# Scale and shift of every modulation in two halves of the columns, in a four-stream transformer kernel

## The chip, the cores and the metric

The kernel runs on one core of one Trainium2 chip. The metric is the device time of one execution in microseconds. TensorE is called PE in the rows (PEld its weight loads), VectorE DVE, ScalarE ACT, GpSimd POOL and SyncE SP.

## The reference

The input `x` is 128 sequences of 32 tokens of 128 features; `cond` is one row of 128 features for each sequence. Four layers follow one another. Layer 0 is a graph attention in two directions over the first 20 tokens as keys. Layers 1 and 3 each have an attention block and an MLP block with 512 hidden features; layer 2 has two MLP blocks, with 128 and 256 hidden features. Each of these six blocks begins with a layer norm and a modulation whose scale and shift come from `cond`:

```
xn = _layernorm(x, g, be)
xm = xn * (1.0 + sc[:, None, :]) + sh[:, None, :]
x  = x + gt[:, None, :] * block(xm)      # attention, or gelu(xm @ W1 + b1) @ W2 + b2
```

## The kernel before

The 128 sequences are cut into 8 chunks of 16 sequences, 512 tokens each (`C` = 512 columns, `NB` = 16 sequences of `S` = 32). Four streams (`NS` = 4) have their own buffers and PSUM banks; stream s does chunk s and then chunk s + 4. All matrices are fp32.

Every engine has a list of stages written out as a string of digits in `MERGE`: each digit says which stream's next stage comes (4 is the setup). An engine takes its list strictly in order and waits on semaphores; so a stage that waits holds up all that is behind it on that engine. Six blocks (`BLOCKS`, index 0 to 5; 0 and 4 are attention, 1, 2, 3 and 5 are MLPs) make 48 modulations in the 8 chunks, 32 of them for MLPs.

The way of one chunk through the beginning of a block:

- `stats` on VectorE (L886 to L893), then on GpSimd the reciprocal root (L637) and L639
- `norm` on ScalarE, four 128x128 activations (L736), each transposed by TensorE into the bank `xn` (L1037)
- `modulate` on VectorE (L899): features times scale, 128x512, from PSUM into the tile `turned_in` (called `xm0` here)
- `modulate` on GpSimd (L644): plus shift, into the tile `xm`. For an attention block the columns are written in another order (`keys_order`)
- on TensorE, for an MLP, `hidden` u = 0, 1, ... (L1058): 128x512 matmuls of one weight tile each, two passes in the trace, so that the 88 hidden matmuls are 176 entries; for an attention block `keys` (q at L973, k at L976) and `vals` (L981)
- GELU on ScalarE (L741), `down` on TensorE (L1067, 32 entries for 512 hidden features), gate and residual on VectorE (L905, L908). GpSimd adds the gated bias to x in `base` (L623).

In attention, TensorE does many small matmuls (`scores` L1009, `values` L1024), VectorE adds, takes maxima and subtracts (L847, L851, L854, L856) and transposes (L862), ScalarE does the exponentials (L727), and the divide by the row sums is L866 and L870. ScalarE loads another function table where exp, gelu and tanh-gelu follow one another; such a load is named ACT_TABLE_LOAD at the line of the activation that needs it.

Of the kernel before, what the change touches and what calls it, by code (L numbers as in the profile page):

```python
# [10 lines left out]
ALU = mybir.AluOpType  # L11
# [3 lines left out]
P = 128  # L15
B, S, D = 128, 32, 128
# [130 lines left out]
def order(engine, merge):  # L147
# [2 lines left out]
    return [next(turns[int(s)]) for s in merge]  # L150

MERGE = {
    "tensor": ("001014414042420420132021030023021022201210212122011212121230230023023132323013113203022223321003"
               "231313120132000010113231132230120303321332021300102312310123021020230112100333012022213220331212"
               "312103200001032020230132021311201120302102113201333033021301230210113231310303102313031333310112"
               "210023213303012122223012100003303213111101302023331331201222030101123132020201320331302211232031"
               "33123021202103321323010000013111313333"),
    "vector": ("001014441442204200330120220201200212212201202210121011312012213233231023203032033301332321302011"
               "130112231303023303122310021033101023122023321102210023020233100132012101031133120021132320233203"
               "112022332020122033021001100100313013321123131313133013223300021302211102031303322113010332013102"  # L160
               "01232310122310021103323122023320031221132013013303011203310313"),
    "scalar": ("444444041440440412440212000312222001112221122303202013333201102332222103213301230010023111103223"
               "021330332210031023211002310201133022322101332212300010320220201310113200012113333120301211323031"
               "330302123310110321330122202231300002131101130231333021223010211302120302332101320133123230221230"
               "10003011113333"),
    "gpsimd": ("001102132042003122020112220211220123000133311213322332330232001211022003231302112200310311300301"
               "212233112230030332001112221010332030231321200212213003130031031311313133232200021110320203310121"
               "22300121133021023002331113332322010031133"),
    "sync": ("041200022211123033321203120312023102301201320123021302210231003103111323330123021031023120132031"
               "230123013"),  # L170
}
ORDERS = {engine: order(engine, merge) for engine, merge in MERGE.items()}

# [75 lines left out]
def build(nc, t_in, out):  # L249
    with ExitStack() as ctx:  # L250
# [149 lines left out]
        def by_seq(a):  # L400
            return a.rearrange("p (q n) -> p q n", n=S)

        def keys_order(a):
            return a.rearrange("p (b t n) -> p t b n", b=BT, t=T)

        def as_seqs(a):
            return a.rearrange("p (t b n) -> p t b n", t=T, b=BT)
# [4 lines left out]
        def count(c, per, k):  # L412
            return c // NS * per + k
# [19 lines left out]
        for j_, a_ in ATTN_OF_BLOCK.items():  # L433
            READ[f"oT a{a_}"] = (oT_ready, 2, a_ - 1)
        for j_ in range(NBLK):
            READ[f"xn{j_}"] = (scaled, NBLK, j_ + 1)
            READ[f"y{j_}"] = (x_ready, NBLK + 1, j_ + 2)
            for u_ in range(BLOCKS[j_][2]):
                READ[f"h{j_}.{u_}"] = (h_ready, NHID, HIDDEN_BEFORE[j_] + u_ + 1)
# [59 lines left out]
        def _(sp):  # L499
# [22 lines left out]
            def stage(kind, a, c):  # L522
                s = c % NS
                if kind == "vals":
                    sp.wait_ge(v_ready[s], count(c, NATT, a + 1))
                    sp.wait_ge(kbd_pool[s], count(c, NATT, a + 1))
                    if a:
                        await_fill(sp, c, f"O1 a{a - 1}")
                    elif c == 0:
                        sp.wait_ge(pool_clear, 1)  # L530
                    elif c < NS:
                        sp.wait_ge(cleared, NS + c)
                    for t in range(T):
                        sp.dma_start(vbd[s][S * t:S * t + S, t], v_ev[s][S * t:S * t + S]).then_inc(vbd_loaded[s], 16)
                if kind == "xin":
                    sp.wait_ge(kbd_pool[s], count(c, NATT, 2))
                    sp.dma_start(turned_in[s][:], t_in["x_tok"][c]).then_inc(x_loaded[s], 16)
                if kind == "mod":
                    sp.wait_ge(rows_ready, 1)
                    sp.dma_start(gates.rearrange("b j f -> b (j f)"), gate_rows[:].rearrange("p j k f -> p (j k f)")  # L540
                                 ).then_inc(gates_stored, 16)
                if kind == "gates":
                    if c < NS and a == 0:
                        sp.wait_ge(gates_stored, 16)
                    if c >= NS or a:
                        sp.wait_ge(x_ready[s], count(c, NBLK + 1, a + 1 if a else 0))
                    table = gates[c * NB:(c + 1) * NB, a].rearrange("(t b) f -> b t f", b=BT)
                    for b in range(BT):
                        sp.dma_start(gate[s][S * b:S * b + S].rearrange("n t k f -> n t (k f)"),
                                     table[b].unsqueeze(0).broadcast_to([S, T, 2 * D])).then_inc(gate_loaded[s], 16)  # L550
                if kind == "next_adj":
                    sp.wait_ge(scored[s], count(c, NATT * PAIRS, NATT * PAIRS))
                    load_adj(c + NS)
                if kind == "next_x":
                    sp.wait_ge(xm_ready[s], count(c, NBLK, NBLK))
                    load_x(c + NS)
                if kind == "store":
                    await_x(sp, c, NBLK)
                    sp.dma_start(out[c], x[s][:].rearrange("p t f -> p (t f)")).then_inc(x_stored[s], 16)
# [8 lines left out]
        def _(pool):  # L568
# [17 lines left out]
            def stage(kind, a, c):  # L586
# [51 lines left out]
                    pool.wait_ge(rstd_ready[s], count(c, 2 * NBLK, 2 * a + 1))  # L638
                    pool.tensor_tensor(nmr[s][:], neg_mean[s][:], rstd[s][:], ALU.mult).then_inc(rstd_ready[s], 1)  # L639
                if kind == "modulate":  # L640
                    pool.wait_ge(scaled[s], count(c, NBLK, a + 1))
                    shift = mod[:, 2 * a + 1, c * NB:(c + 1) * NB].rearrange("p (t b) -> p t b", b=BT)
                    turned_out = keys_order(xm[s][:]) if BLOCKS[a][0] == "attn" else as_seqs(xm[s][:])
                    pool.tensor_tensor(turned_out, as_seqs(xm0[s][:]), shift.unsqueeze(3).broadcast_to([P, T, BT, S]), ALU.add  # L644
                                       ).then_inc(xm_ready[s], 1)

            for kind, a, c in ORDERS["gpsimd"]:
                stage(kind, a, c)
# [100 lines left out]
        def _(dve):  # L749
# [48 lines left out]
            def stage(kind, a, c):  # L798
# [95 lines left out]
                if kind == "modulate":  # L894
                    await_fill(dve, c, f"xn{a}")
                    if c < NS:
                        dve.wait_ge(mod_ready, a + 1)
                        dve.wait_ge(mod_summed, a + 1)
                    dve.tensor_tensor(by_seq(xm0[s][:]), by_seq(bank(s, f"xn{a}")), seqs(mod[:, 2 * a], c), ALU.mult  # L899
                                      ).then_inc(scaled[s], 1)  # L900
                if kind in ("project", "down"):
                    await_fill(dve, c, f"y{a}")
                    dve.wait_ge(gate_loaded[s], count(c, 16 * BT * NBLK, 16 * BT * (a + 1)))
# [11 lines left out]
        def _(pe):  # L915
# [14 lines left out]
            def stage(kind, a, c):  # L930
# [32 lines left out]
                if kind == "keys":  # L963
                    if a == 0:
                        pe.wait_ge(sf_ready[s], count(c, 2, 1))
                    if a >= 2:
                        pe.wait_ge(xm_ready[s], count(c, NBLK, 1 if a == 2 else 5))
                    if c < NS and a == 0:
                        pe.wait_ge(graph_loaded, 16)
                    if c < NS and a >= 2:  # L970
                        pe.wait_ge(w_loaded[1 if a == 2 else 3], 16)
                    await_bank(pe, c, f"q a{a}")
                    pe.matmul(bank(s, f"q a{a}"), q_weight(a), src[:], start=True, stop=True).then_inc(filled[s], 1)  # L973
                    await_bank(pe, c, f"k a{a}")
                    n = width(a)
                    pe.matmul(bank(s, f"k a{a}")[:, 0:NB * n].rearrange("p (q m) -> p q m", m=n), k_weight(a),  # L976
                              by_seq(src[:])[:, :, 0:n], start=True, stop=True).then_inc(filled[s], 1)
# [72 lines left out]
                    last.then_inc(filled[s], 1)  # L1050
                if kind == "hidden":
                    j, u = divmod(a, UNITS)
                    if u == 0:
                        pe.wait_ge(xm_ready[s], count(c, NBLK, j + 1))
                        if c < NS and j == 2:
                            pe.wait_ge(w_loaded[2], 16)
                    await_bank(pe, c, f"h{j}.{u}")
                    pe.matmul(bank(s, f"h{j}.{u}"), w[UP[j]][:, 0, u * D:(u + 1) * D], xm[s][:], start=True, stop=True  # L1058
                              ).then_inc(filled[s], 1)
                if kind == "down":  # L1060
                    nh = BLOCKS[a][2]
                    for u in range(nh):
# [55 lines left out]
```

## Time and profile before

| what | value |
|---|---|
| median of 3 runs | 586.82 us (585.61 to 589.59) |
| the profiled execution, its own time | 584.34 us |
| its span, first to last instruction | 582.6 us |
| mean granted TensorE clock | 0.909 of full |
| busy PE, DVE, ACT, POOL | 490.1, 460.5, 367.5, 316.2 us |
| instructions | 23163 |

Busy time is the time in which an engine had an instruction under way. The span is 1.7 us under the execution's own time.

### The profile page before, as it was taken

The numbers are of one execution on the slowest core, as the hardware profiler recorded it, in microseconds if no ns is written. First come the engines' busy times: TensorE is split into PE (matmuls) and PEld (weight loads), VectorE is DVE, ScalarE is ACT, GpSimd is POOL, SyncE is SP. The second block draws the span as 40 slices with busy tenths as digits, with TensorE's granted clock in tenths as the row PEclk, the third lists the DMA queues.
The fourth block names the chain that finished last, engine by engine and source line by source line (L and its number), as shares of the span: only waits on it lengthen the run. The fifth ranks groups of instructions, "written<-read, shape, count | busy, mean of one in ns | idle before, by whom it ended". The sixth has DMA issues, their size and how long they took to land.

```text
span 582.6 us, 23163 instructions
## 1 busy us (share of the span) xinstructions
PE 490.1 (84%) x10086; PEld 340.5 (58%) x10086; DVE 460.5 (79%) x1091; ACT 367.5 (63%) x598; POOL 316.2 (54%) x326
## 2 busy tenths in 40 slices
PE   4798658879889889689999898756889999887997
PEld 1465545656466565556667566544658666565755
DVE  5689798987886657989989876769988677899941
ACT  5865325754596759758868656522577468966652
POOL 4877356643463654685676546444353767834150
PEclk9989868898799896999999999675999999997899
DMA  8723411240232432525425413130132344422130
GB/s 293 304 89 100 125 24 35 48 120 3 74 94 60 123 96 85 135 76 151 124 78 136 105 31 84 37 98 4 24 95 72 84 128 118 115 59 61 50 97 37
DMA packets 40117, 53.51 MB, mean 92 GB/s; under 512 B 5840, under 2 KB 30672, under 8 KB 40016
## 3 DMA queue, kind: packets, MB, share of 16 engines
q1 hardware_dynamic: 39552, 51.14, 31.1%
q8 instruction: 80, 1.31, 1.0%
q10 hardware_dynamic: 432, 0.88, 0.4%
q0 software_dynamic: 32, 0.01, 0.3%
q14 instruction: 21, 0.17, 0.1%
HBM read 39.68 MB, written 2.88 MB: 73 GB/s over the span
## 4 chain that ended last, share of the span: by engine, by line
PE 48%; DVE 23%; issue 11%; POOL 10%; ACT 6%; DMA 1%; ACTq 0%; POOLq 0%; DVEq 0%
PE work L1067 10%; PE work L1058 10%; PE work L1009 8%; PE work L1024 6%; PE work L973 4%; DVE prob L862 3%; DVE stats L886 3%; PE work L976 3%; POOL xm L644 2%; PE work L981 2%; DVE mx L854 2%; DVE work L905 2%; POOL rstd L637 2%; DVE x L908 2%; DVE prob L856 2%
## 5 line engine op out<-in xcount | busy, mean ns | idle before, releaser
L736 ACT ACTIVATE xn<-x,nmr,rstd 128x128 f32<-128x128 f32 x192 | 79.0, 486 | 41.6 <-POOL nmr L639 41.4
L1058 PE MATMUL work<-xm,w_layer 128*128 128x512 f32 x176 | 94.9, 659 | 6.6 <-POOL xm L644 5.1
L1009 PE MATMUL work<-kbd,qT 32*32 32x80 f32 (+1 forms) x4096 | 73.6, 270 | 24.7 <-issue 17.2
L741 ACT ACTIVATE prob<-work,first 128x512 f32<-128x512 f32 x88 | 59.0, 686 | 50.5 <-PE work L1058 50.4
L727 ACT ACTIVATE prob<-prob 128x640 f32<-128x640 f32 (+1 forms) x64 | 57.5, 898 | 50.2 <-POOL prob L629 39.0
L1067 PEld LDWEIGHTS work<-w_layer,prob 128*128 128x128 f32 x704 | 82.0, 193 | 11.7 <-ACT prob L741 8.8
L1067 PE MATMUL work<-w_layer,prob 128*128 128x128 f32 x704 | 85.6, 279 | 3.0 <-ACT prob L741 2.9
L637 POOL TENSOR_TENSOR rstd<-veps,neg_half 128x4 f32<-128x4 f32 x48 | 48.9, 1018 | 66.2 <-DVE veps L893 66.2
L1009 PEld LDWEIGHTS work<-kbd,qT 32*32 32x32 f32 x4096 | 59.2, 110 | 42.7 <-issue 30.2
L644 POOL TENSOR_TENSOR xm<-turned_in,mod 128x512 f32<-128x512 f32 x48 | 50.7, 1058 | 54.5 <-DVE turned_in L899 54.5
L862 DVE STREAM_TRANSPOSE prob<-prob 128x1024 f32<-128x1024 f32 x64 | 77.2, 1227 | 2.5 <-ACT prob L727 2.5
L611 POOL TENSOR_TENSOR kbd<-turned_in,head_mask 128x640 f32<-128x640 f32 (+1 forms) x32 | 50.4, 1576 | 51.3 <-ACT turned_in L704 51.3
L1024 PE MATMUL work<-vbd,prob 128*32 128x36 f32 x4096 | 54.2, 210 | 20.4 <-issue 11.4
L1024 PEld LDWEIGHTS work<-vbd,prob 128*32 128x32 f32 x4096 | 47.3, 119 | 40.6 <-issue 27.4
L905 DVE TENSOR_TENSOR work<-work,gate 128x512 f32<-128x512 f32 x48 | 33.3, 694 | 45.0 <-PE work L1067 40.3
L629 POOL TENSOR_TENSOR prob<-prob,mx 128x640 f32<-128x640 f32 x32 | 41.8, 1309 | 37.4 <-DVE mx L851 37.4
L623 POOL TENSOR_TENSOR x<-x,gate 128x512 f32<-128x512 f32 x48 | 61.0, 1274 | 0.0
L1058 PEld LDWEIGHTS work<-xm,w_layer 128*128 128x128 f32 x176 | 31.2, 205 | 37.1 <-ACT prob L741 14.9
L1037 PE MATMUL work<-ident,xn 128*128 128x128 f32 x192 | 38.3, 309 | 5.6 <-ACT xn L736 4.6
L854 DVE TENSOR_REDUCE mx<-work 128x32 f32<-128x1024 f32 x32 | 38.8, 1211 | 5.1 <-PE work L1009 4.9
L886 DVE BATCH_NORM_STATS2 stats<-x 128x6 f32<-128x128 f32 x192 | 41.6, 280 | 1.0
L708 ACT ACTIVATE kbd<-work,kb_head,head_mask 128x320 f32<-128x320 f32 (+1 forms) x64 | 41.3, 703 | 0.2 <-DVE edge L830 0.2
(128 smaller groups left out, 828.6 us busy)
## 6 DMA issues: line engine op xcount, KB each, us to landing
gate<-gates SPq DMA_DIRECT2D x192, 128.0 KB, 3.3
vbd<-v_ev SPq DMA_DIRECT2D x128, 72.0 KB, 2.5
kbd<-in_adj SPq DMA_DIRECT2D x8, 704.0 KB, 6.5
turned_in<-in_x_tok SPq DMA_DIRECT2D x8, 256.0 KB, 2.9
out_x<-x SPq DMA_DIRECT2D x8, 256.0 KB, 2.1
turned_in<-in_x_feat SPq DMA_DIRECT2D x7, 256.0 KB, 4.6
w_layer<-in_weights SPq DMA_DIRECT2D x2, 768.0 KB, 14.2
prob<-in_modw SPq DMA_DIRECT2D x1, 768.0 KB, 10.9
```

The lines of the kernel that those rows point to most:

```text
L623: pool.tensor_tensor(x[s][:], x[s][:], gate[s][:, :, 1], ALU.add).then_inc(based[s], 1)
L637: pool.tensor_tensor(rstd[s][:], veps[s][:], neg_half[:], ALU.pow).then_inc(rstd_ready[s], 1)
L644: pool.tensor_tensor(turned_out, as_seqs(xm0[s][:]), shift.unsqueeze(3).broadcast_to([P, T, BT, S]), ALU.add).then_inc(xm_ready[s], 1)
L727: act.activation(e, e, ACT.Exp).then_inc(exped[s], 1)
L736: act.activation(xn[s][:, t], x[s][:, t], ACT.Identity, scale=rstd[s][:, t:t + 1], bias=nmr[s][:, t:t + 1]).then_inc(xn_ready[s], 1)
L741: act.activation(hT[s][u], bank(s, f"h{j}.{u}"), GELU[BLOCKS[j][3]], bias=vec(HID_BIAS[j], u)).then_inc(h_ready[s], 1)
L862: dve.transpose(e, e).then_inc(turned[s], 1)
L886: dve.bn_stats(stats[s][:, t], x[s][:, t]).then_inc(dve_step[s], 1)
L1009: last = pe.matmul(to[:, b * GH * n:(b + 1) * GH * n], qT[s][rows_g, q * S:(q + 1) * S], kbd[s][rows_g, :, q * n:(q + 1) * n], start=(a != ...
L1024: last = pe.matmul(out_h[S * b:S * b + S, :, i * GH + h], prob[s][:, PG * pair + i, b * GH + h], vbd[s][:, :, b * H + (PG * pair + i) * GH ...
L1058: pe.matmul(bank(s, f"h{j}.{u}"), w[UP[j]][:, 0, u * D:(u + 1) * D], xm[s][:], start=True, stop=True).then_inc(filled[s], 1)
L1067: last = pe.matmul(bank(s, f"y{a}")[:, t * D:(t + 1) * D], hT[s][u][:, t * P:(t + 1) * P], w[DOWN[a]][:, u], start=(u == 0 and t == 0), st ...
```

## The change

The scale on VectorE and the shift on GpSimd are issued as two instructions each, one for columns 0 to 255 and one for columns 256 to 511, and `scaled` and `xm_ready` count both. GpSimd waits for each half of the scale by itself. For an MLP the first hidden projection (u = 0) is two matmuls of 256 columns, each waiting for its half of the shift; the others stay whole. An attention block's projections wait for both halves. SyncE's load of the next chunk waits for both halves of the last block. All five `MERGE` lists are different.

```diff
 MERGE = {
-    "tensor": ("001014414042420420132021030023021022201210212122011212121230230023023132323013113203022223321003"
...
+    "tensor": ("010104414042440130132101302110013031021032002111303300230232210321123021022003301000231231300121"
...
-            READ[f"xn{j_}"] = (scaled, NBLK, j_ + 1)
+            READ[f"xn{j_}"] = (scaled, 2 * NBLK, 2 * j_ + 2)
...
-                    sp.wait_ge(xm_ready[s], count(c, NBLK, NBLK))
+                    sp.wait_ge(xm_ready[s], count(c, 2 * NBLK, 2 * NBLK))
...
                 if kind == "modulate":
-                    pool.wait_ge(scaled[s], count(c, NBLK, a + 1))
                     shift = mod[:, 2 * a + 1, c * NB:(c + 1) * NB].rearrange("p (t b) -> p t b", b=BT)
                     turned_out = keys_order(xm[s][:]) if BLOCKS[a][0] == "attn" else as_seqs(xm[s][:])
-                    pool.tensor_tensor(turned_out, as_seqs(xm0[s][:]), shift.unsqueeze(3).broadcast_to([P, T, BT, S]), ALU.add
-                                       ).then_inc(xm_ready[s], 1)
+                    for k in range(2):
+                        ts = slice(k * T // 2, (k + 1) * T // 2)
+                        pool.wait_ge(scaled[s], count(c, 2 * NBLK, 2 * a + k + 1))
+                        pool.tensor_tensor(turned_out[:, ts], as_seqs(xm0[s][:])[:, ts],
+                                           shift[:, ts].unsqueeze(3).broadcast_to([P, T // 2, BT, S]), ALU.add
+                                           ).then_inc(xm_ready[s], 1)
...
-                    dve.tensor_tensor(by_seq(xm0[s][:]), by_seq(bank(s, f"xn{a}")), seqs(mod[:, 2 * a], c), ALU.mult
-                                      ).then_inc(scaled[s], 1)
+                    scale = seqs(mod[:, 2 * a], c)
+                    for k in range(2):
+                        dve.tensor_tensor(half_seqs(xm0[s][:], k), half_seqs(bank(s, f"xn{a}"), k),
+                                          scale[:, k * NB // 2:(k + 1) * NB // 2], ALU.mult).then_inc(scaled[s], 1)
...
-                        pe.wait_ge(xm_ready[s], count(c, NBLK, 1 if a == 2 else 5))
+                        pe.wait_ge(xm_ready[s], count(c, 2 * NBLK, 2 if a == 2 else 10))
...
-                    if u == 0:
-                        pe.wait_ge(xm_ready[s], count(c, NBLK, j + 1))
-                        if c < NS and j == 2:
-                            pe.wait_ge(w_loaded[2], 16)
+                    if c < NS and j == 2 and u == 0:
+                        pe.wait_ge(w_loaded[2], 16)
                     await_bank(pe, c, f"h{j}.{u}")
-                    pe.matmul(bank(s, f"h{j}.{u}"), w[UP[j]][:, 0, u * D:(u + 1) * D], xm[s][:], start=True, stop=True
-                              ).then_inc(filled[s], 1)
+                    parts = 2 if u == 0 else 1
+                    for k in range(parts):
+                        if u == 0:
+                            pe.wait_ge(xm_ready[s], count(c, 2 * NBLK, 2 * j + k + 1))
+                        at = slice(k * C // parts, (k + 1) * C // parts)
+                        last = pe.matmul(bank(s, f"h{j}.{u}")[:, at], w[UP[j]][:, 0, u * D:(u + 1) * D], xm[s][:, at],
+                                         start=True, stop=True)
+                    last.then_inc(filled[s], 1)
```

## Rows read from the trace of the kernel before

**Rows 1.** The page: busy time of each engine, share of the span, instructions

```profile
PE 490.1 (84%) x10086; PEld 340.5 (58%) x10086; DVE 460.5 (79%) x1091; ACT 367.5 (63%) x598; POOL 316.2 (54%) x326
```

**Rows 2.** The page's 40 slices: granted clock in tenths of full

```profile
PEclk9989868898799896999999999675999999997899
```

**Rows 3.** The page: the chain that ended last, by engine

```profile
PE 48%; DVE 23%; issue 11%; POOL 10%; ACT 6%; DMA 1%; ACTq 0%; POOLq 0%; DVEq 0%
```

**Rows 4.** Windows, 343.1 to 431.2 us: length, busy times, then clock

```profile
343.10:431.20 88.10, 66.66 (x2186) 48.76 (x2184) 72.78 (x144) 43.20 (x71) 41.30 (x41) 0.81 0.22 55
```

**Rows 5.** Waits: engine, who waited for whom, us in total, times, longest

```profile
PE work L1058 <- POOL xm L644: 5.1, 6, 2.0
```

**Rows 6.** The chain in order of time, shifts (start us, us, what)

```profile
180.84 1.00 POOL xm L644
181.84 1.23 POOL x L623
...
250.19 2.77 issue
252.96 1.06 POOL xm L644
...
487.33 1.06 POOL xm L644
```

**Rows 7.** The chain in order of time, scales

```profile
130.59 0.68 DVE turned_in L899
...
534.80 0.69 DVE turned_in L899
```

**Rows 8.** Groups of instructions: scale and shift (busy us, mean ns, idle before)

```profile
L644 POOL TENSOR_TENSOR xm<-turned_in,mod 128x512 f32<-128x512 f32 x48 | 50.7, 1058 | 54.5 <-DVE turned_in L899 54.5
...
L899 DVE TENSOR_TENSOR turned_in<-work,mod 128x512 f32<-128x512 f32 x48 | 32.4, 681 | 8.5 <-PE work L1037 8.3
```

**Rows 9.** Groups of instructions: smaller ones of the same kind

```profile
L870 DVE TENSOR_TENSOR xn<-work,recip 128x256 f32<-128x256 f32 x48 | 18.1, 420 | 0.8
...
L639 POOL TENSOR_TENSOR nmr<-neg_mean,rstd 128x4 f32<-128x4 f32 x48 | 9.7, 202 | 3.8
...
L815 DVE TENSOR_TENSOR gate_rows<-work,gate 128x128 f32<-128x128 f32 x6 | 1.7, 277 | 2.0 <-ACT mod L688 2.0
```

**Rows 10.** Timeline, 554 to 557.2 us: one MLP's modulation in the last blocks

```profile
554.11 0.68 DVE L899 TENSOR_TENSOR turned_in<-work,mod 128x512 f32<-128x512 f32 x1
...
554.87 1.05 POOL L644 TENSOR_TENSOR xm<-turned_in,mod 128x512 f32<-128x512 f32 x1 [0.97 <-DVE turned_in L899]
...
555.97 3.89 PE L1058 MATMUL work<-xm,w_layer 128*128 128x512 f32 x8
...
557.13 0.69 ACT L741 ACTIVATE prob<-work,first 128x512 f32<-128x512 f32 x1 [1.55 <-PE work L1058]
```

**Rows 11.** Timeline, 556.5 to 559.9 us: weight loads and down matmuls

```profile
556.50 0.19 PEld L1058 LDWEIGHTS work<-xm,w_layer 128*128 128x128 f32 x1 [0.24 <-issue]
556.93 0.19 PEld L1058 LDWEIGHTS work<-xm,w_layer 128*128 128x128 f32 x1 [0.24 <-issue]
...
559.87 3.81 PE L1067 MATMUL work<-w_layer,prob 128*128 128x128 f32 x32
```

**Rows 12.** Timeline, 458.3 to 458.6 us: a scale beside a shift

```profile
458.35 1.05 POOL L644 TENSOR_TENSOR xm<-turned_in,mod 128x512 f32<-128x512 f32 x1
458.51 0.69 DVE L899 TENSOR_TENSOR turned_in<-work,mod 128x512 f32<-128x512 f32 x1 [0.88 <-PE work L1037]
```

**Rows 13.** Groups of instructions: table loads on ScalarE

```profile
L741 ACT ACT_TABLE_LOAD x22 | 28.2, 1283 | 0.4
...
L727 ACT ACT_TABLE_LOAD x15 | 19.2, 1283 | 0.3
```

**Rows 14.** The chain in order of time: first and last of six table loads

```profile
162.41 1.28 ACT L741
...
311.17 1.28 ACT L741
```

More of the change, by code:

```diff
@@ L152 @@
 MERGE = {
-    "tensor": ("001014414042420420132021030023021022201210212122011212121230230023023132323013113203022223321003"
[L154 to L170, printed above, removed]
+    "tensor": ("010104414042440130132101302110013031021032002111303300230232210321123021022003301000231231300121"
+               "320320133101133221120203003133123321022223001330111022320133030110213221230131311322123003003011"
+               "320112010132120131320320310331201300310303220231103210313212320322113200320233222022121213201330"
+               "130032211230120300132001231112112032003331323210221223001303121120200313303102112230012030313123"
+               "12103232003003210231233211213123222322"),
@@ new lines @@
+    "vector": ("001014444144032310130011201021030002010111033130122123032132002022202332030313023112311001321033"
+               "312302202331012320102330112321303121002320103302013112121301213300133110320322311233202020123130"
+               "201201030031031010302231131013123233220321232132220030212023012110331032311220120323101232001233"
+               "01123210032310122310332000130121201312033301312323212032221232"),
+    "scalar": ("444444401440404441410320011110330221032103330022210312031200102310030231203213012311102300132331"
+               "032223210301120320133201132210133123132200003111210320101321330300201311331200223333211022230302"
+               "222012231013310231202310200301211101320133233021223210032110230103320110322101332310322003010223"
+               "13321113232222"),
@@ L171 @@
+    "gpsimd": ("001102134030110132021032010313020012313211220300232333220100110300133211022301301312032213321131"
+               "220303320211001221133303310022021113220033310103201300222312213113233220220011103001332022113001"
+               "33211022301033120123213332202020131133222"),
+    "sync": ("014001101323303222103201031203120301231012331021032103120030113213332202221302103120312031203123"
+               "021302132"),
 }
@@ L401, in by_seq, with half_seqs @@
             return a.rearrange("p (q n) -> p q n", n=S)
+        def half_seqs(a, k):
+            return by_seq(a)[:, k * NB // 2:(k + 1) * NB // 2]
         def keys_order(a):
```

## The prediction

> **What bounds the kernel now.** I read the engine table first. TensorE (PE) is busy 84% of the span and VectorE (DVE) 79% [rows 1]: two engines near their limit, neither at it. The slices show TensorE's granted clock dipping now and then [rows 2]. The chain that ended last splits its time among PE 48%, DVE 23%, issue 11%, POOL (GpSimd) 10% and ScalarE (ACT) 6% [rows 3]. So the end is set by a path that hops between engines in the order that the lists give. The windows show where it is worst. From 343.1 to 431.2 us, the stretch between two MLP matmul groups while all four streams are in attention, PE is busy 66.66 of 88.1 us at a granted clock of 0.81 of full (that is, partly at the 1.2 GHz level instead of 2.4) [rows 4].
>
> Then I looked at how the scale and the shift lie on the path. PE's own queue waited for a shift before a hidden matmul 5.1 us in 6 places [rows 5]. That is the whole of PE idleness that ends on the MLP's modulate. The chain shows 14 shifts. I followed each to its next piece: five go to hidden matmuls (252.96 and 487.33 are the first and last of them), four to a q projection, five to more GpSimd work (180.84 is the first) [rows 6]. The pieces called "issue" or "POOLq" ahead of several of these, such as the one ahead of 252.96, are GpSimd waiting, at the end for the scale. Of the scales themselves nine stand on the chain. Eight of them are followed by other VectorE work (first 130.59, last 534.80) [rows 7], that is, they are there because VectorE's queue was full, not because their own result was awaited.
>
> **The change, part by part.**
>
> *Scale in halves (48 times).* Now one 128x512 takes 681 ns, the mean of 48 [rows 8]. VectorE tensor_tensor with a PSUM input at 128x256 took 420 ns (48 of the 64 divides) and at 128x128 277 ns [rows 9]. The line through 277 and 681 puts 256 columns at 277 + 128 x 1.052 = 412 ns, so 420 fits. Two halves are 840 ns: +0.16 us each, +7.6 us of VectorE work in 48. What is on the path is less: eight scales in its queue, 8 x 0.16 = 1.3 us. Bounds: 23% (its share of the chain) of 7.6, 1.7 us, sits near this; the whole 7.6 us if VectorE becomes the bound; and 0 if the others wait for something else. I take 1.3.
>
> The Trainium skill ("VectorE: DVE Perf Modes", the section on the TRN2 errata) speaks against the edit: every instruction pays a fixed cost, and it advises tiles of at least 512 elements. It gives (N+151)/0.96 ns for an fp32 tensor_tensor, an estimate of 691 ns for 512 and 424 for 256, near the rows just named; read as a rule for the whole kernel it would make all 48 penalties count, the third case below.
>
> *Shift in halves (48 times).* 1058 ns now [rows 8]. No 256-column GpSimd add is in the trace. From below, the 128x4 tensor_tensor takes 202 ns [rows 9]; the straight line from it to 1058 gives 202 + 252 x (1058 - 202)/508 = 627 ns, two 1254, so +0.20 us each and +9.4 us in 48. The bound below is half of 1058 (no fixed cost), +0; above, each half costs all 202 more than its share, (529 + 202) x 2 = 1.46, +0.40. I take +0.20, as the 128x4 is the same kind of instruction. On the chain eight shifts touch GpSimd's own queue (five followed by GpSimd work, and three of those ahead of a q projection that follow GpSimd work): 8 x 0.20 = 1.6 us, between 0 and 3.2.
>
> *Latency.* The last MLPs show one modulate by itself: scale 554.11, shift 554.87, hidden matmul 555.97, GELU 557.13 [rows 10], 3.02 us from scale to GELU. With halves: scale half 0.42, hand-over 0.08 (554.11 + 0.68 to 554.87), two shift halves 1.25, hand-over 0.05, then only the second matmul half. A hidden projection is two fp32 passes whose weight loads start 0.43 apart [rows 11], so 0.86 us for 512 columns and 0.43 for 256. The first half's matmul runs under the second shift half, so 1.16 - 0.43 = 0.73 remains after the last shift. Sum 2.53, a gain of 0.49 us for each MLP. In attention blocks q waits for both halves, and only 0.68 + 1.06 - (0.42 + 1.25) = 0.07 us is gained. On the path: 5 x 0.49 = 2.5 us for the hidden ones and at most 0.1 for attention. The upper bound is that all 32 MLPs count within their four streams, 8 x 0.49 = 3.9 us a stream, plus what the queue wait of 5.1 us [rows 5] could give: between 0 and 5.
>
> The overlap itself needs scale and shift side by side at full speed. At 458.35 a shift ran 1.05 us with a scale of 0.69 us beside it from 458.51 [rows 12], each near its mean; no contention to price.
>
> *First projection as two matmuls (32 times).* Each half of 256 columns is 2 passes of 0.21 us, and its weight load is 0.19 us [rows 11], which just hides. PE cost: 0, at most 32 x 2 x 0.19 = 12 us if none of the added loads hid. I take 0, since the 128-column matmuls of the down projection run 32 passes in 3.81 us, 0.12 us each, with the same loads [rows 11]. PE now stands at two waits instead of one. Behind it in its queue wait other streams' matmuls, but the second wait ends 0.07 us earlier than the single one did.
>
> *Waits and queues.* The load of the next chunk (SyncE, next_x) waits for 12 halves instead of 6 shifts: the same moment less 0.07 us, no cost. The bank of xn is released after the second scale, 0.16 us later; the next fill of that bank is a hidden unit 1, or v in attention, which comes after the shift, so this is hidden under about 1.3 us of shift. The softmax reduction queued behind a scale on VectorE is what pays, already counted.
>
> *The orders.* This is the largest edit: every engine's list is different. Two things can be counted in them. First, ScalarE reloads its table when exp, gelu and tanh-gelu alternate. Walking the old list gives 37 changes after the first load, and the trace has 22 + 15 = 37, each 1283 ns [rows 13]. The new list gives 45: +8 loads, +10.3 us of ScalarE. On the chain there are 6 of the 37 (first 162.41, last 311.17) [rows 14], so 8 x 6/37 x 1.28 = 1.7 us, between 0 and 10.3. Second, the middle stretch of PE's list without an MLP stage shrinks from 59 stages to 52. It is the stretch of 88.1 us above; if it shrinks in proportion, 7/59 x 88.1 = 10.5 us leave it. But the attention stages that leave go into other stretches where PE is busy too, so I price it at 0 and keep 10.5 as the bound of the gain. At the end stream 2 is last; between its project (block 4) and its norm (block 5) stand two hidden matmuls and one down, 2 x 0.86 + 3.81 = 5.5 us of PE work. That covers, bar about 1 us, the way round from project to norm. I put +1 us for the tail, where today PE has no gap from 555.97 on.
>
> *Sum.* -2.5 - 0.1 (latency) + 1.3 (VectorE) + 1.6 (GpSimd) + 0 (matmuls) + 1.7 (tables) + 0 (middle) + 1 (tail) = +3.0 us. Against the profiled execution, 584.3 us, this is 587.3. That execution is 2.5 us under the median of the three others, 586.8, which would give 589.8. Of these two I take 588, since one of the three (585.6) is also near the profile. The runs spread over 4 us, so less than 1% (5.9 us) counts here as no difference.
>
> **The rivals.** *A, the new lists fill the valley.* For: PE is idle a quarter of the 88.1 us and its clock is low there, and 7 fewer stages without an MLP between; more alternating tables mean that MLPs and attention are mixed more. Against: DVE is busy through much of that stretch anyway. Price: half to all of 10.5 us and the full latency gain of 5: 587 - 5 to 587 - 15.5, middle 577 us.
>
> *B, VectorE becomes the bound.* The place is attention, where scales stand in a full queue. For: eight of nine scales on the chain are queued; with each split, VectorE's 460.5 us become 468. Price: all 7.6 us of scales, and half the table loads, 5 us, less 2 of latency, 586.8 + 10.6 = 597 us. It decides from the point where the VectorE penalty reaches the path in more than 2.5 / 0.16, some 16 of 48, instead of 8.
>
> *C, the halves do not overlap.* GpSimd comes to the first half only when the second is done too, because its own queue is late. Then nothing is gained and only its +0.20 are paid: +5.5, 592 us, at the edge of no difference.
>
> **How the numbers follow.** The forecast (no difference, 588) has 0.34, and C 0.08, of which half counts as slower. A has 0.30: the lists were changed so much that half of what they do can't be read from counts. B has 0.28. Faster by over 1% 0.30, within 1% 0.38, slower by over 1% 0.32. The range takes in A's middle nearly and B's: 575 to 600. The forecast's own range is 581 to 593.
>
> **What would show it.** Scale halves at 420 ns, x96; shift halves near 627 ns, x96; 45 table loads besides the first; the first hidden GELU of an MLP 2.5 us after the scale starts. In the waits, PE's wait for a shift before a hidden matmul falls from 5.1 us to about 3. If A holds, the middle stretch without MLP matmuls is shorter than 80 us and its clock above 0.81. If B holds, DVE's share of the chain rises past 27%. I am wrong if the middle or the tail moves by over 6 us, or if the shift halves cost 0.73 us each.

## The result and the profile after

The changed kernel takes 594.67 us (median of 4, 592.57 to 596.58), the kernel before 586.22 in the same comparison: a ratio of 1.0136 with a 95% interval of 1.0075 to 1.0197. It is slower, by about 8 us. The profiled execution took 593.38 us, its span is 591.4 us. Medians and ranges in this document are of all executions of a kernel, while ratios and their intervals leave out those more than 1.5% above the kernel's fastest.

The page of the changed kernel: busy time by engine and the chain by engine.

```profile
PE 491.8 (83%) x10150; PEld 357.2 (60%) x10150; DVE 460.8 (78%) x1139; ACT 375.1 (63%) x606; POOL 323.0 (55%) x374
...
PE 49%; DVE 20%; POOL 10%; issue 10%; ACT 9%; DMA 1%; SPq 0%; DVEq 0%; POOLq 0%; ACTq 0%
```

Against [rows 1] VectorE's busy time did not move (460.5 to 460.8), though it has 48 instructions more. GpSimd has 6.8 us more, ScalarE 7.6, TensorE 1.7. The span grew by 8.8. So no engine's work grew by what the kernel lost (on TensorE 7.1 of the 8.8 us are idle time), and VectorE's share of the chain fell, from 23% [rows 3] to 20%.

The groups of instructions of the changed kernel: busy us, mean ns of one, idle before.

```profile
L649 POOL TENSOR_TENSOR xm<-turned_in,mod 128x256 f32<-128x256 f32 x96 | 57.4, 620 | 41.5 <-DVE turned_in L907 41.5
...
L907 DVE TENSOR_TENSOR turned_in<-work,mod 128x256 f32<-128x256 f32 x96 | 35.6, 412 | 5.6 <-PE work L1045 5.4
L747 ACT ACT_TABLE_LOAD x27 | 34.6, 1283 | 0.5
...
L733 ACT ACT_TABLE_LOAD x18 | 23.1, 1283 | 0.3
```

The recorded time of each half is what the prediction gave it, the scale 412 ns and the shift 620, and there are 45 table loads. But 96 scales of 412 would be 39.6 us, and the group was busy 35.6. So the recorded times of the two halves of a pair overlap. Compared with [rows 8], the split costs VectorE 3.2 us, not 7.6, and GpSimd 6.7, not 9.4.

The timeline of the changed kernel near its end, one MLP's modulation, the counterpart of [rows 10].

```profile
575.01 0.74 DVE L907 TENSOR_TENSOR turned_in<-work,mod 128x256 f32<-128x256 f32 x2
...
575.50 1.19 POOL L649 TENSOR_TENSOR xm<-turned_in,mod 128x256 f32<-128x256 f32 x2 [2.74 <-DVE turned_in L907]
...
576.27 3.08 PE L1069 MATMUL work<-xm,w_layer 128*128 128x256 f32 x8 [0.57 <-POOL xm L649]
...
577.48 0.69 ACT L747 ACTIVATE prob<-work,first 128x512 f32<-128x512 f32 x1 [1.07 <-PE work L1069]
```

A pair of scales takes 0.74 us, a pair of shifts 1.19. The first hidden matmul starts while the second shift is still under way, and GELU starts 2.47 us after the first scale (577.48 - 575.01) where it was 3.02. At this place the mechanism works as it is meant to, and a little better than the forecast 2.53.

A wait of the changed kernel (us in total, times, longest) and the middle stretch without MLP matmuls, 351.8 to 435.9 us, in a window.

```profile
PE work L1069 <- POOL xm L649: 4.5, 7, 1.3
```

```profile
351.80:435.90 84.10, 62.94 (x1911) 43.39 (x1910) 64.96 (x136) 39.03 (x67) 39.85 (x45) 0.82 0.17 44
```

The wait before a hidden matmul fell only from 5.1 [rows 5] to 4.5 us. The wait of a q projection (L973, now L981) for its shift grew from 8.0 to 10.5 us. The middle stretch shrank from 88.1 [rows 4] to 84.1 us at nearly the same clock (0.81 and 0.82), and still the kernel is slower. So the loss is not in that stretch.

### The profile page after: what moved, and what is told of

Its sections match the earlier page's. It is cut to its first block, busy times and chain, and to the rows that moved or that the text cites. A ratio compares the mean times of both kernels' runs of the same rounds, so it can differ in the third digit from the quotient of the medians.

```text
span 591.4 us, 23395 instructions
## 1 busy us (share of the span) xinstructions
PE 491.8 (83%) x10150; PEld 357.2 (60%) x10150; DVE 460.8 (78%) x1139; ACT 375.1 (63%) x606; POOL 323.0 (55%) x374
## 4 chain that ended last, share of the span: by engine, by line
PE 49%; DVE 20%; POOL 10%; issue 10%; ACT 9%; DMA 1%; SPq 0%; DVEq 0%; POOLq 0%; ACTq 0%
PE work L1069 10%; PE work L1079 9%; PE work L1017 7%; PE work L1032 5%; PE work L981 4%; PE work L989 4%; PE work L984 4%; DVE prob L868 3%; POOL xm L649 3%; DVE mx L860 3%; DVE x L916 2%; DVE work L913 2%; DVE stats L892 2%; DVE prob L862 2%; POOL kbd L614 2%
## 5 line engine op out<-in xcount | busy, mean ns | idle before, releaser
L1069 PE MATMUL work<-xm,w_layer 128*128 128x256 f32 (+1 forms) x240 | 94.3, 519 | 4.6 <-POOL xm L649 4.5
L1017 PE MATMUL work<-kbd,qT 32*32 32x80 f32 (+1 forms) x4096 | 75.0, 276 | 21.9 <-issue 16.2
L649 POOL TENSOR_TENSOR xm<-turned_in,mod 128x256 f32<-128x256 f32 x96 | 57.4, 620 | 41.5 <-DVE turned_in L907 41.5
L1032 PE MATMUL work<-vbd,prob 128*32 128x36 f32 x4096 | 52.7, 208 | 22.6 <-issue 11.9
L1069 PEld LDWEIGHTS work<-xm,w_layer 128*128 128x128 f32 x240 | 43.3, 203 | 24.1 <-issue 13.2
## 6 DMA issues: line engine op xcount, KB each, us to landing
prob<-in_modw SPq DMA_DIRECT2D x1, 768.0 KB, 10.9
```

Source lines behind the costliest of these rows:

```text
L649: pool.tensor_tensor(turned_out[:, ts], as_seqs(xm0[s][:])[:, ts], shift[:, ts].unsqueeze(3).broadcast_to([P, T // 2, BT, S]), ALU.add).th ...
L1017: last = pe.matmul(to[:, b * GH * n:(b + 1) * GH * n], qT[s][rows_g, q * S:(q + 1) * S], kbd[s][rows_g, :, q * n:(q + 1) * n], start=(a != ...
L1032: last = pe.matmul(out_h[S * b:S * b + S, :, i * GH + h], prob[s][:, PG * pair + i, b * GH + h], vbd[s][:, :, b * H + (PG * pair + i) * GH ...
L1069: last = pe.matmul(bank(s, f"h{j}.{u}")[:, at], w[UP[j]][:, 0, u * D:(u + 1) * D], xm[s][:, at], start=True, stop=True)
```

## Experiments

Two things were changed together, the split of the instructions and the lists. The first pair takes them apart. L stands for the lists, S for the split.

**Split, old lists.**

```diff
-MERGE = { five new strings }
+MERGE = { the five strings of the kernel before }
```

> The changed kernel with the five lists of the kernel before; all three splits stay. If the lists cost the time (theory L), this is at most 0.5% off the kernel before, 583 to 589 us, and perhaps faster, since 5 hidden waits on the chain shrink by 0.49 us. If the added instructions cost it (theory S), it is 1.2 to 1.6% slower, 593 to 596 us, with VectorE's share of the chain above 23%.

Measured: 0.9996 of the kernel before, interval 0.9956 to 1.0036. The split by itself costs and gains nothing that can be seen. The plain mean of its 11 executions other than the profiled one is 587.9 us, against 586.5 for 28 of the 29 of the kernel before (the other took 610.28), so a cost of 0.2 to 0.4% is not excluded. The profiled execution took 638.12 us at a granted clock of 0.717, so its rows are not read.

**No split, new lists.**

```diff
-MERGE = { the five strings of the kernel before }
+MERGE = { five new strings }     # nothing else of the change
```

> The kernel before, no split, with the five new lists. Theory L: slower by 1.4% or more, 594 us and up, since the lists were laid out for the halves and lack them here. Theory S: within 0.5% of the kernel before, 583 to 589 us.

Measured: 1.0130, interval 1.0078 to 1.0182, 593.56 us. That is the whole loss of the changed kernel (1.0136). Theory L, which expected 1.4% or more, holds but for 0.1%, and S falls: the lists cost 1.3% whether or not the instructions are split.

The page of the run with new lists and no split, and one of its waits:

```profile
PE 495.2 (84%) x10086; PEld 345.4 (59%) x10086; DVE 458.3 (78%) x1091; ACT 374.8 (64%) x606; POOL 316.4 (54%) x326
...
PE 43%; DVE 20%; POOL 17%; issue 12%; ACT 8%; SPq 0%; DMA 0%; POOLq 0%; DVEq 0%; ACTq 0%
```

```profile
PE work L1058 <- POOL xm L644: 9.5, 13, 1.9
```

The span is 589.4 us, 6.8 longer than before. TensorE's busy time, for the same 10086 entries, is 5.1 us longer and its idle time 1.7 us (589.4 - 495.2 against 582.6 - 490.1). On the chain GpSimd takes 17% and VectorE 20%, against 10% and 23%. It is another path through the engines.

This run is also the right base for the waits. Under the new lists TensorE waits 9.5 us in 13 places for a shift before a hidden matmul, against 5.1 in 6 places under the old ones [rows 5], and the split brings that down to 4.5 us in 7. So the split does take 5 us of these waits away, and the kernel is no faster for it (1.0136 against 1.0130): here, a wait of TensorE that went was not time that the kernel gained.

*Where along the run?* The order of VectorE's list tells which modulation each scale belongs to. The last scale of the first four chunks (block 5) starts at 326.28 us under the old lists and at 326.42 under the new ones. Work done up to there, before and in this run (length, then busy time of PE, PEld, DVE, ACT, POOL, then the clock):

```profile
0.00:326.28 326.28, 273.30 (x5735) 186.93 (x5736) 266.51 (x610) 214.83 (x345) 191.60 (x196) 0.91 0.37 108
```

```profile
0.00:326.42 326.42, 271.91 (x5484) 188.79 (x5488) 259.63 (x602) 208.84 (x341) 188.20 (x194) 0.89 0.36 105
```

The first four chunks come no later to their last modulation, but 6.9 us less of VectorE's work is done by then: the chunks that follow are less advanced. Over the whole run VectorE's idle time is 9.0 us longer, and 7.0 of these lie ahead of that point. In the changed kernel, whose last scale of the first round starts at 325.75, it is 5.7 of 8.6. These are single executions, and they say where VectorE's idle time has grown, not why.

**Is it the table loads?** The new lists have 45 loads after the first instead of 37. Two kernels do without any.

```diff
-        GELU = {"Gelu": ACT.Gelu, "Gelu_apprx_tanh": ACT.Gelu_apprx_tanh}
+        GELU = {"Gelu": ACT.Identity, "Gelu_apprx_tanh": ACT.Identity}
```

> The kernel before with both GELUs replaced by the identity function, so that ScalarE loads no table between them and the exponentials (the nonlinearity is left out, shapes and order are the same). 37 loads of 1.28 us go. If loads on the chain count as in the prediction (6 of 37), it falls by about 8 us, to 578. If all count, by 40 us or more.

> The changed kernel with both GELUs replaced by the identity function, as in the run beside it. 45 loads go. If the 8 added loads are what costs (theory T), the gap to the other identity kernel is under 3 us; if they are hidden, it stays at 7 to 10 us, as between the two full kernels.

Measured: 1.0014 (0.9972 to 1.0056) for the old lists, 1.0085 (1.0048 to 1.0123) for the changed kernel. Both expectations for the first miss: with all 37 loads gone it gained nothing, not 8 us and not 40. By the lower end of the interval it can have gained 1.6 us at most. The page of each, engine busy time, of the old lists first.

```profile
PE 496.4 (85%) x10086; PEld 343.8 (59%) x10086; DVE 460.2 (79%) x1091; ACT 318.2 (54%) x561; POOL 316.1 (54%) x326
```

```profile
PE 495.7 (84%) x10150; PEld 360.1 (61%) x10150; DVE 460.2 (78%) x1139; ACT 317.1 (54%) x561; POOL 322.9 (55%) x374
```

ScalarE lost 49 and 58 us of work, 367.5 to 318.2 and 375.1 to 317.1, and the time hardly moved. So the six loads on the chain of before [rows 14] did not hold up the end. That behind each stood other work that came nearly as late is the likely reason, but no run shows which work. The mean granted clock of the executions in the ratio, 0.902 against 0.905 before, is too near to have eaten a gain of 8 us. The gap between the two identity kernels is 0.7% where the full ones have 1.36%, about 4 us of 8, give or take 3. That lies between what the two theories expected (under 3 us, and 7 to 10). About half of the loss is there without a single load; whether the 8 added loads cost the other half is not decided.

**Is it the tail?** The new lists end with stream 2's chunk 6 alone. Both sets of lists were cut short, without the split.

```diff
+# in every list, for chunks 4 to 7: no stats, norm, modulate, base, hidden, down and gates of block 5
-                    await_x(sp, c, NBLK)
+                    await_x(sp, c, NBLK if c < NS else NBLK - 1)
```

> The kernel before without block 5 (the last MLP) of chunks 4 to 7: that block's stages are dropped from every list, the result is that after block 4. The last 20 us or so go, to about 562 us. Base of the comparison with the next run.

> The same cut with the new lists and whole scale, shift and projection. If the new lists lose their time in the last blocks (theory T: the tail with stream 2 last), the gap to the old lists falls from 7.7 us to under 3. If the loss is spread over the whole run (theory W), 5 us or more remain.

Measured: 560.56 us (0.9582, interval 0.9514 to 0.9650) and 571.46 us (0.9745, interval 0.9659 to 0.9830). The ratios are 1.6% apart, 9.5 us, and by the two intervals the gap lies between 3 and 16 us. (The medians are 10.9 us apart, with one of the four executions with new lists at 578.18; the spans of the two profiled ones are only 4.4 us apart.) So the gap doesn't go away with the last MLPs, which speaks against the tail theory, if narrowly. Stream 2 is still the last one in the cut kernel, now with its block 4, so a cost of that order is not ruled out.

The traces of the full kernels give the tail a size: in the last 40 us TensorE is idle 4.6 us before, 6.6 in the changed kernel and 6.8 with the new lists alone. That is 2 us of the 8.

**The first half alone.**

```diff
+# in every list only the setup and chunks 0 to 3; no next_adj, no next_x
-                sp.wait_ge(x_stored[s], 16 * (NCH // NS))
+                sp.wait_ge(x_stored[s], 16)
```

> The kernel before with chunks 0 to 3 alone (chunks 4 to 7 and their loads are left out), old lists. About 325 us. Base of the comparison with the next run.

> Chunks 0 to 3 alone, whole stages, new lists. Theory W: the new lists are slower here too, by 3 us or more. Theory T: within 1.5 us of the old ones.

Measured: 323.18 us (315.23 to 326.39, 4 runs) and 326.70 us (326.30 to 326.93). The medians are 3.5 us apart, as theory W (spread over the run) expects. But the four executions with old lists lie at 315.23, 321.07, 325.3 and 326.39, so the gap is anything from nothing to 11 us, and this pair settles nothing.

**What the split is made of.** Its cost and its gain were separated under the old lists.

```diff
-                    parts = 2 if u == 0 else 1
+                    parts = 1
...
-                            pe.wait_ge(xm_ready[s], count(c, 2 * NBLK, 2 * j + k + 1))
+                            pe.wait_ge(xm_ready[s], count(c, 2 * NBLK, 2 * j + 2))
```

> Old lists, scale and shift in halves, but the first projection one matmul that waits for both halves. The added VectorE and GpSimd work stays and most of the earlier start goes (0.43 of the 0.49 us of each MLP). If that start is what pays for the added work, this is 2 to 3 us slower than the kernel before (1.004 to 1.005); if neither matters, 1.000.

Measured: 1.0072, interval 1.0032 to 1.0111, some 4 us slower where 2 to 3 were expected; the interval, 1.9 to 6.5 us, takes them in. With the first projection in halves it was 0.9996. Waits and groups of this run:

```profile
PE work L1069 <- POOL xm L649: 5.4, 7, 1.6
```

```profile
L649 POOL TENSOR_TENSOR xm<-turned_in,mod 128x256 f32<-128x256 f32 x96 | 57.4, 620 | 48.9 <-DVE turned_in L907 48.7
...
L907 DVE TENSOR_TENSOR turned_in<-work,mod 128x256 f32<-128x256 f32 x96 | 35.5, 413 | 8.0 <-PE work L1045 7.9
```

The added work on VectorE and GpSimd is the same as in the changed kernel (35.5 and 57.4 us). So it does reach the end, and the earlier start of the first projection pays it back. At the MLP near the end GELU starts 2.96 us after the first scale here, where it was 2.47 with the projection in halves. The two runs were not taken side by side, each ratio is against its own executions of the kernel before, and the two intervals just overlap (1.0032 against 1.0036), so the size of the repayment, 0.8%, is less certain than its sign.

**More of the same.**

```diff
-                    for k in range(2):
-                        ts = slice(k * T // 2, (k + 1) * T // 2)
-                        pool.wait_ge(scaled[s], count(c, 2 * NBLK, 2 * a + k + 1))
+                    for k in range(4):
+                        ts = slice(k * T // 4, (k + 1) * T // 4)
+                        pool.wait_ge(scaled[s], count(c, 4 * NBLK, 4 * a + k + 1))
...
-                            pe.wait_ge(xm_ready[s], count(c, 2 * NBLK, 2 * j + k + 1))
+                            pe.wait_ge(xm_ready[s], count(c, 4 * NBLK, 4 * j + 2 * k + 2))
```

> Old lists, scale and shift in four quarters each, the first projection still in halves. Against the run with halves and old lists (0.9996) it adds two more scales and two more shifts to each of 48 modulations. If the added fixed costs are on the path (theory S), 1.01 or more; if they are hidden or paid back by the overlap, within 0.5%.

Measured: 1.0120, interval 1.0065 to 1.0176. The timeline near the end and the groups of this run:

```profile
564.29 0.87 DVE L907 TENSOR_TENSOR turned_in<-work,mod 128x128 f32<-128x128 f32 x4
564.65 1.47 POOL L649 TENSOR_TENSOR xm<-turned_in,mod 128x128 f32<-128x128 f32 x4 [0.56 <-DVE turned_in L907]
...
567.07 0.69 ACT L747 ACTIVATE prob<-work,first 128x512 f32<-128x512 f32 x1 [1.29 <-PE work L1069]
```

```profile
L649 POOL TENSOR_TENSOR xm<-turned_in,mod 128x128 f32<-128x128 f32 x192 | 71.0, 404 | 45.6 <-DVE turned_in L907 45.6
...
L907 DVE TENSOR_TENSOR turned_in<-work,mod 128x128 f32<-128x128 f32 x192 | 41.7, 279 | 9.7 <-PE work L1045 9.5
```

Each further instruction adds (0.87 - 0.74)/2 = 0.065 us on VectorE and (1.47 - 1.19)/2 = 0.14 us on GpSimd. The way from scale to GELU is 2.78 us, longer than the 2.47 of halves. GpSimd's 71.0 us are 20.3 over the 50.7 of whole shifts, VectorE's 41.7 are 9.3 over 32.4. At this size it comes out as theory S expects, 1.01 or more: the added costs outrun what the overlap saves. A first projection in quarters too, which might save more, was not tried.

**How far can lists go?** A third set of lists was laid out by moving single entries, each move judged by a rough sum of durations.

```diff
-MERGE = { five new strings }
+MERGE = { a third set }
```

> The changed kernel with a third set of lists, found by moving single entries for a shorter estimated end (34 table changes, longest stretch without an MLP stage on TensorE 53). If the lists are what sets the time (theory L), it can leave both kernels behind by 2 to 5%, 560 to 575 us. If the engines' work sets it, it stays within 1% of 586.

> The same third set of lists with whole scale, shift and projection. Theory L: within 1% of the run beside it, since the split is worth little under any lists. If the split matters more when the lists are good, it is 3 us or more slower than that run.

Measured: 1.1223 (1.1150 to 1.1296) with the split and 1.1187 (1.1099 to 1.1276) without. That the lists set the time holds, in the wrong direction: 12% slower where 2 to 5% faster was hoped for, and the split again makes no difference beyond the noise of about 1%. A wait and the chain by engine of the split one:

```profile
POOL x L626 <- DMA gate<-gates: 43.1, 8, 9.6
```

```profile
PE 45%; DVE 18%; issue 10%; SPq 8%; DMA 8%; POOL 5%; ACT 5%; POOLq 0%; DVEq 0%; ACTq 0%
```

GpSimd's `base` stood 43.1 us waiting for gate rows, where it had no wait before, and SyncE's queue and its DMAs are 16% of the chain, where they were 1% before [rows 3]. In the kernel before, four such DMAs keep that queue for 1.73 us:

```profile
556.14 1.73 SPq L549 DMA_DIRECT2D gate<-gates  x4
```

That is 0.43 us each, and lists laid out with too little for them would come out tight around that queue. But SyncE's queue also stood waiting for x at these gate DMAs, 176.8 us against 141.4 before, and a list that puts them in a bad place would do the same. Neither was tested.

## Why the prediction held, and where it did not

The forecast was 588 within 575 to 600, likeliest no difference; 594.67 lies in the range, 1.1% above the forecast, on the side that had 0.32. The range was 25 us wide, and it holds by its width: the sum gave +3.0 us, the kernel lost 8. Point by point:

- *Scale in halves*: 412 ns a piece as forecast. The term was mis-sized: two halves overlap, so a pair is 0.74 us against 0.68, and all 48 cost 3.2 us of VectorE instead of 7.6. By the Trainium skill ("VectorE: DVE Perf Modes", the section on the TRN2 errata) each split would add 157 ns, an estimate; the trace shows 60 to 67 (0.74 - 0.68 in the timeline, 3.2 us in 48). The figure in the Trainium skill ("Vector Engine (DVE) Microarchitecture Reference", section 5.2 on measured stream behaviour), about 75 ns for each instruction after queue overlap, given there for streams of integers, is near the trace.
- *Shift in halves*: 620 ns against 627. A pair is 1.19 us, +0.14, and all 48 cost 6.7 us instead of 9.4.
- *Latency*: 2.47 us against 2.53, at the one place read. Right there.
- *First projection as two matmuls*: 2 x 0.21 us forecast for 256 columns, no added PE work; the busy time of all hidden matmuls went from 94.9 us to 94.3, and TensorE's as a whole from 490.1 to 491.8. Right. It pays back what the added work costs, 1.0072 against 0.9996.
- *The three together*: -2.6 + 1.3 + 1.6 = +0.3 us forecast; measured -0.2 us, with an interval from -2.6 to +2.1. Right as a sum. Its terms are less sure: the added work alone cost about 4 us, where the same terms gave some 2.5, and the repayment looks larger by as much, so two errors may cancel.
- *Table loads*: 45, as counted. The price of 1.7 us was worked out from their share of the chain. Under the old lists all 37 together cost nothing that can be seen (1.0014); under the new ones removing all gave some 3 us, not clear of noise. A share of the chain was taken for a price, and that was the fault.
- *The middle stretch*: 4.0 us shorter, about 40% of the 10.5 that proportion gave, and it did not shorten the kernel, as the sum had assumed. Rival A, which wanted it under 80 us and at a higher clock, did not come true.
- *The tail*: +1 us forecast. TensorE's idle time in the last 40 us grew by 2, and the runs without the last MLPs kept a gap of 3 to 16 us, so most of the loss is likely not there.
- *The lists as a whole*: this is the step that failed. The sum gave them 1.7 + 0 + 1 = +2.7 us, and they cost 1.3%, some 7.6 us, by themselves. Rival B's 597 us is nearest to the measured time, but by luck: its mechanism, VectorE becoming the bound, did not come true. VectorE's share of the chain fell to 20% where B wanted over 27, its busy time stayed, and the split that B blames cost nothing that can be seen.
- *C, no overlap*: did not happen at the place read; the timeline shows the first projection starting under the second shift.

What stays open is why the new lists lose. It is not the split, about half of it is there without any table load, and the last 40 us show 2 us of it on TensorE. Most of VectorE's added idle time lies in the first 326 us. The busy time of TensorE grew by 5.1 us for the same matmuls in the run without the split, its mean clock was 0.904 against 0.909, and its idle time by 1.7; no run separates these.

## What to carry to other kernels

When a change comes with a new hand-laid order, run the order and the code change separately first: here the order was 1.3% and the code change nothing beyond 0.4%. Then compare waits with the run that has the same order: against the kernel before the split seemed to save 0.6 us of hidden waits, under the same lists it saved 5, and neither shortened the kernel. A share of the chain that ended last is not a price: taking 49 us of work off ScalarE, six pieces of it on that chain, gave nothing. Splitting an instruction for overlap has its own cost (0.14 us for each further piece on GpSimd here). In this kernel halves broke even only with the first projection split too (1.0072 without), and quarters of scale and shift lost 1.2%.

## What the runs showed of the hardware

Two adjacent VectorE instructions of 256 columns, 412 ns each, took 0.74 us together, and four of 128 columns, 279 ns each, 0.87 us: in a row, one more instruction costs about 0.065 us, not the 0.14 us that the durations of single ones suggest (2 x 412 - 681 = 143). On GpSimd the same step costs 0.14 us (1.05, 1.19 and 1.47 us for one, two and four pieces).
